# Decoder layer, second stage: convolution units in two bursts of three, the eight turns in one burst

## What is computed

```python
x = layernorm(x + attention(x))                      # 32 heads, causal, rope
x = layernorm(x + conv3(x, similarity(ctx_4096)))    # 3 taps along the features
x = layernorm(x + ffn(x))                            # 8 adapters of rank 16, gated by a softmax
# conv3: out[o, t] = sum over c, k of weight[o, c, k] * x_pad[c, t + k] * att[c, k, t]
# ffn:   2 * sum over h, r of (x A[h, r]) * B[h, :, r] * 8 softmax(x Wr + br)[h]
```

## Time and profile before

| | |
|---|---|
| runs of the kernel | 1407.62, 1408.07, 1410.24 us |
| profiled execution, span | 1404.9 us |
| its own time | not listed apart from the span |
| TensorE matmul busy | 1359.3 us, 97% |
| VectorE, POOL, ScalarE busy | 1094.9, 984.3, 931.8 us |
| chain that ended last | TensorE 87% |

### The profile page before, as it was taken

The page is one execution under the profiler, slowest core; times in us unless marked ns, Lnnn a source line. Parts: engine busy times, 40 slices in busy tenths (PEclk is TensorE's granted clock), DMA queues, the critical chain, the costliest instruction groups (busy, mean ns, idle before and its releaser), DMA issues.

```text
span 1404.9 us, 32306 instructions
## 1 busy us (share of the span) xinstructions
PE 1359.3 (97%) x8294; PEld 1058.0 (75%) x8294; DVE 1094.9 (78%) x3869; ACT 931.8 (66%) x3258; POOL 984.3 (70%) x936
## 2 busy tenths in 40 slices
PE   8999999999999999999986999999999999999995
PEld 6777777777777777777754788888888888888873
DVE  5887887878788787787775678887788877888774
ACT  5888888878788887888884455554555545555443
POOL 4777776777777677777774667766777667776653
PEclk9999999999999999999998999999999999999997
DMA  7354545445453544545478865657656666676751
GB/s 264 96 152 123 159 116 158 128 136 159 114 159 117 155 137 129 159 115 164 124 208 242 181 162 157 166 153 171 157 157 165 156 171 156 160 161 158 157 120 45
DMA packets 108861, 213.03 MB, mean 152 GB/s; under 512 B 26640, under 2 KB 32272, under 8 KB 108816
## 3 DMA queue, kind: packets, MB, share of 16 engines
q1 hardware_dynamic: 108480, 211.73, 56.5%
q10 hardware_dynamic: 336, 0.79, 0.2%
HBM read 131.83 MB, written 34.47 MB: 118 GB/s over the span
## 4 chain that ended last, share of the span: by engine, by line
PE 87%; POOL 3%; DMA 2%; SPq 2%; DVE 2%; issue 2%; ACT 2%; ACTq 0%; DVEq 0%; POOLq 0%
PE wo_ps L479 34%; PE wo_ps L1134 23%; PE conv_ps L1145 9%; PE s_ps L509 5%; PE pv_ps L522 4%; PE ffn_ps L1167 4%; PE ffn_ps L1179 3%; PE ffn_ps L1160 2%; PE turn_ps L498 2%; SPq L320 1%; POOL prods L1488 1%; ACT pexp L767 1%; DMA pt<-in_wqkv 1%; DMA raw<-in_xT 1%; PE turn_ps L488 0%
## 5 line engine op out<-in xcount | busy, mean ns | idle before, releaser
L479 PE MATMUL wo_ps<-weights,halves 128*128 128x512 f32 x2304 | 570.7, 400 | 3.5 <-DVE weights L681 3.5
L479 PEld LDWEIGHTS wo_ps<-weights,halves 128*128 128x128 f32 x2304 | 422.8, 189 | 137.8 <-issue 53.8
L767 ACT ACTIVATE pexp<-sm,smin 128x128 f32<-128x128 f32 x1024 | 398.0, 391 | 99.0 <-DVE smin L618 98.0
L1134 PE MATMUL wo_ps<-weights,halves 128*128 128x512 f32 x1464 | 393.2, 401 | 1.0 <-PEq L143 1.0
L1488 POOL TENSOR_TENSOR prods<-prod,prods 128x512 fp32r<-128x512 f32 x192 | 259.3, 1359 | 131.0 <-ACT prods L1382 126.0
L906 POOL TENSOR_TENSOR pn<-pexp,prec 128x512 f32<-128x512 f32 x256 | 265.4, 1041 | 98.1 <-DVE prec L625 98.1
L1134 PEld LDWEIGHTS wo_ps<-weights,halves 128*128 128x128 f32 x1464 | 267.1, 189 | 58.1 <-issue 1.8
L618 DVE CUSTOM_DVE_ANT_0 sm<-s_ps,mask_t 128x128 f32<-128x128 f32 x1024 | 231.9, 282 | 24.9 <-PE s_ps L509 19.6
L1382 ACT CAST prods<-prod 128x512 fp32r<-128x512 f32 x192 | 118.9, 621 | 165.5 <-DVE prod L1271 127.9
L1271 DVE TENSOR_TENSOR prod<-att,x 128x512 f32<-128x512 f32 x192 | 186.6, 987 | 13.3 <-DMA att<-sim_scratch 8.4
L767 ACT ACTIVATION_READ_ACCUMULATOR pexp<-sm,smin 128x1 f32 x1024 | 193.4, 189 | 0.0
(11 more groups left out here) (103 smaller groups left out, 1636.5 us busy)
## 6 DMA issues: line engine op xcount, KB each, us to landing
att<-sim_scratch SPq DMA_DIRECT2D x192, 252.0 KB
pt<-blocks SPq DMA_DIRECT2D x636, 64.0 KB, 2.0
ctx_t<-in_ctx SPq DMA_DIRECT2D x32, 576.0 KB, 5.2
raw<-in_xT SPq DMA_DIRECT2D x32, 512.0 KB, 3.9
xn<-in_x SPq DMA_DIRECT2D x32, 512.0 KB, 7.6
out<-late SPq DMA_DIRECT2D x32, 512.0 KB, 6.2
ot_scratch<-ot SPq DMA_DIRECT2D x63, 256.0 KB, 2.1
raw<-ot_scratch SPq DMA_DIRECT2D x31, 512.0 KB, 6.8
```

The source lines that it names most:

```text
L479: mm = pe.matmul(qkv_ps[(par + g) % 2][:], xs[:, par, xl, k], w_sb[:, wl, g, k], start=(k == 0 and n == 0), stop=(k == KT - 1 and n == 2))
L767: ins = nc.scalar.activation(pexp[:, c % 2, i * P:(i + 1) * P], sm[:, c % 2, i * P:(i + 1) * P], ACT.Exp, bias=smin[:, c % 2, i:i + 1], sc ...
L1134: mm = pe.matmul(wo_ps[n][:], os_t[:, par, ol, k], wo_sb[:, wl, k, n * BANK:(n + 1) * BANK], start=(k == 0 and m == 0), stop=(k == KT - 1 ...
```

## The change

The slots of the units become 13 for units 0 to 2 and 20 (slot 4 of the next step) for units 3 to 5; both turns go to slot 12. Since several units share a slot, the loop goes over all units in each slot. The tail gets unit 3 of sequence 30, which the last step no longer issues. Nothing changes on the other engines, and the waits stay.

```diff
-    CONV_AT = (9, 11, 13, 15, 17, 20)
+    CONV_AT = (13, 13, 13, 20, 20, 20)
...
             for s in range(SLOTS2):
-                if valid(f) and s + SLOTS2 in conv_at(f):
-                    convolve(f, conv_at(f).index(s + SLOTS2))
-                if valid(c) and s in conv_at(c):
-                    convolve(c, conv_at(c).index(s))
+                for m in range(UNITS):
+                    if valid(f) and conv_at(f)[m] == s + SLOTS2:
+                        convolve(f, m)
+                    if valid(c) and conv_at(c)[m] == s:
+                        convolve(c, m)
...
                 if valid(f):
-                    if s in (11, 12):
-                        turn_x2(f, par, s - 11)
+                    if s == 12:
+                        turn_x2(f, par, 0)
+                        turn_x2(f, par, 1)
...
         steps(pe, step, 0, B - 1, LEAD, TAIL - 3)
 
+        convolve(B - 2, 3)
         convolve(B - 2, 4)
         turn_low(B - 3)
         convolve(B - 2, 5)
```

## The result

The changed kernel takes 1423.03 us (median of four runs, 1420.61 to 1423.79) against 1408.72 for the kernel before (median of four, the three listed above and one more): the ratio is 1.0096, with a 95% interval of 1.0082 to 1.0109. That is 14.3 us slower. Forecast were 1418.2 us, 10.1 us slower, in a range of 1412.5 to 1426.5: the direction and the mechanism came out, the size fell short by 4 us.

What follows compares the result with a forecast made beforehand. TensorE's always-busy queue was taken to bound the kernel, at 19.52 us a step. The terms 11.9 - 0.9 - 0.2 - 0.7 = +10.1 us on 1408.07 gave 1418.2 us, range 1412.5 to 1426.5.

Steps and rivals of the forecast that it cites:

- The wait at the expansion: TensorE's expansion load waits for low_lt, losing 0.41 us a step over 29 steps: +11.9 us, bounds 11.3 and 17.7.
- The add's start: VectorE's add(c, 0, 1), starting low_lt's chain, begins right behind gate_low, between 1011.63 and 1011.72, taken as 1011.65.
- The edges: Joining TensorE's groups of units and turns saves 0.03 us a step (0 to 0.17): -0.9 us, bounds 0 and -5.
- The other waits: Turns, both bursts and turn_low come earlier but keep their margins (0.4, 0.1 and 0.2 us where given): no cost.
- Behind the last step: In the tail everything hangs on add(31, 0, 1), which comes 0.7 us earlier: -0.7 us, bounds 0 and -0.8.
- Step 2: Unit 0's 0.54 us wait goes, but the turns meet normalise2 and take the gain away: -0.2 us, bounds 0 and -1.3.
- 1 (a second wait at reduce_rank): Unit 0 reaches ScalarE late, delaying reduce_rank: 0.3 us a step more, 9 us, 1427 us; chance 0.12.
- 2 (the edges pay): Joined groups gain the whole 0.17 us a step, the wait costs 0.17 or less: 1407 us; chance 0.06.
- 3 (the clock falls): TensorE's stop each step drops its clock to 0.93, regular steps some 7% longer, 38 us: 1456 us; chance 0.03.

Runs made afterwards that it cites:

- experiment 5: The changed kernel with the expansion moved from slot 3 to slot 4, ahead of the burst there: 1407.04 us, ratio 0.9995 to the kernel before.
- experiment 6: The changed kernel with VectorE's low_lt ahead of average(c, 0) instead of behind it: 1408.23 us, ratio 0.9995 to the kernel before.
- experiment 2: The kernel before with only units 3 to 5 at slot 4 of the next step, units 0 to 2 and turns unmoved: 1420.98 us, ratio 1.0103.
- experiment 3: The kernel before with unit 4 alone moved from slot 1 to slot 4 of the next step: 1418.19 us, ratio 1.0085.
- experiment 11: The kernel before with an unread VectorE maximum over 384 columns added just ahead of low_lt: 1416.68 us, ratio 1.0063.
- experiment 7: The changed kernel with VectorE's second-stage loop written out for all 32 steps: 1419.21 us, ratio 1.0081 to the kernel before.
- Experiment 9: The kernel before with units 0 to 2 at slot 13 and the turns left where they were: 1412.59 us, ratio 1.0035.
- experiment 4: The kernel before with unit 3 alone moved from slot 15 to slot 1 of the next step: 1406.33 us, ratio 0.999.
- experiment 8: The kernel before with units 0 to 2 at slot 13, units 3 and 4 at next step's slot 1, turns at slot 12: 1406.69 us, ratio 0.9991.

## Why the prediction was right, and where it was short

Against the profiled execution the 15.7 us divide so. Up to the start of slot 14 of step 2, its reduce_rank (793.50 us before, 796.13 after), 2.6 us, of which 2.5 were there already at the first convolution unit of sequence 0 (771.57 and 774.04), ahead of everything that the change moves. Some 1.4 us of the 15.7 belong to the two executions, by the medians; whether all of the 2.5 do isn't shown. From there over 29 steps 12.8 us. From slot 14 of step 31 to the end 0.4 us (45.33 before, 45.69 after). So the edit's own part is some 13.3 us, against 14.3 by the medians.

- **The wait at the expansion: right.** Where it lies, whom it waits for and that 29 steps pay it. The size was forecast as 0.41 us. The even steps' 19.88 us are 0.42 above the 19.46 of experiment 5 and 0.39 above the 19.49 of experiment 6, which has the change's own order of TensorE. Experiments 2, 3, 6 and 11 each confirm one piece of that sum: which unit matters, which does not, that the chain's length decides, and what a waiting expansion gives back.
- **The add's start: the step that failed.** "The add therefore starts between 1011.63 and 1011.72 (0.05 for a handover)" left out what VectorE does between gate_low, the last of its step, and the add, the first of the next: in every second step its loop turns there. It takes 0.2 us, and before the change it lay in the add's 0.66 us of idle time. The change used up that idle time. Measured: 0.22 us in 11 steps, 2.4 us; experiment 7 takes it away. The forecast counted the whole 0.66 us as free, and the loop's turn at nothing.
- **The edges: small, as forecast.** Forecast -0.03 us a step, within 0 to -0.17; measured -0.03 in the change's own order (experiment 6) and -0.06 in experiment 5. The 0.36 us that an even step lost in all is the same either way.
- **The other waits: right, with the margins forecast.** No wait at L1160 or L1167 in the regular steps of the changed kernel. Experiment 9 shows how near the first one was.
- **Behind the last step: wrong sign.** Forecast -0.7 us, measured +0.4. That "everything hangs on add(31, 0, 1)" failed: in the tail VectorE's products of sequence 31 stand behind add(30, 1, 1), which waits for unit 5, and unit 5 waits for POOL, whose work did not move with the projection. Rows of the changed kernel:

```profile
1380.02 0.97 PE L1145 MATMUL conv_ps<-prods,weights 128*128 128x512 f32 x3 [0.18 <-POOL prods L1491]
...
1381.03 0.69 DVE L1245 TENSOR_TENSOR y<-conv_ps,x 128x512 f32<-128x512 f32 x1 [0.43 <-PE conv_ps L1145]
```

  The add came right behind low_lt before; now it stands 0.43 us idle. The first product still comes 0.45 us earlier against slot 14 than it did, and the last units 0.2 us later. POOL's first instruction for sequence 30's second norm starts 0.18 us earlier against slot 14, but takes 0.93 us where it took 0.55, and normalise2 behind it is 0.16 us later. That this and a clock of 0.75 to 1.00 there lose the rest is argued from the profile and wasn't tried.
- **Step 2:** forecast -0.2 us, measured about +0.1 to +0.2 (2.63 less 2.47). The turns did meet normalise2, for longer than thought:

```profile
791.73 1.06 PE L1160 MATMUL ffn_ps<-id_t,late 128*128 128x128 f32 x8 [1.12 <-ACT late L1396]
```

- **The rivals.** 1 (a second wait at reduce_rank) did not come: no wait at L1167. 2 (the edges pay) failed, at 0.03 to 0.06 us of gain against 0.39 to 0.42 of loss. 3 (the clock falls) failed: PEclk 1.00 over 28 steps that each stop once. By the rule of the Trainium skill, TensorE: Matmul & The Clock Gate, "A second HAM failure mode: psum-queue depth-cycling", small stops between groups of matmuls can make the clock go up and down; 29 stops of TensorE did not here.

The sum again with what was measured: 29 x 0.36 + 11 x 0.22 = 12.9 us for the 29 steps (12.8 measured), and with +0.2 and +0.4 for the ends 13.5. Against the 10.1 forecast, the loop's turn is 2.4 us of the miss, the part behind the last step 1.1 and step 2 0.4, while the steps themselves lost 0.6 less. The 0.8 us up to the medians' 14.3 are open, within what the runs of one kernel scatter by.

## What to carry to other kernels

In a queue that is always busy, moving work later brings everything behind its old place earlier: list each wait between the old and the new place and ask how far its chain moves along. Work ahead of the chain's start moves both, and cost nothing here but the loop's turn that it laid bare; work between the chain's start and its reader takes its whole length from the margin. Before idle time of another engine is counted as margin, look for what it hides: a loop's turn shows in no row as long as something else is waited for.

## What was not expected of the hardware

- The turn of VectorE's loop takes about 0.22 us between two dependent steps (19.88 and 20.10 us in turn; 19.88 throughout once written out). The Trainium skill, Advanced Engine Details and Errata, "Control Flow Timing", gives about 108 ns for a compare-and-branch; no run here shows the branch apart from the register work around it, and together they are twice that.
- A group of matmuls that had to wait runs through 0.13 us faster from its first load than one in a full queue (1.66 against 1.79 us), so the first 0.13 us of a wait are free. This was read from two rows before, and experiment 11 bears it out: 0.46 us of delay, 0.19 of it within the margin, cost 0.15 and not 0.27.
- Interrupting the projections with other groups of matmuls has a price, but a small one: 0.03 to 0.07 us of a step of 19.5 for one to four interruptions fewer, and not in proportion to their number (one fewer in experiment 4 gave 0.05, three in experiment 6 gave 0.03 and in experiment 8 0.07). What it consists of isn't shown.
